# One of four tiles of the second layer normalisation moved to GpSimd, with new instruction orders at both ends

## The chip, the core and the metric

The kernel runs on one core of a Trainium2 chip, as one program with five engines: TensorE (PE, whose weight loads are shown apart as PEld), VectorE (DVE), ScalarE (ACT), GpSimd (POOL) and SyncE (SP, which here only starts DMAs). The metric is the device time of one execution in microseconds; smaller is better. The kernel before took 207.63 us (median of 3 runs, 207.59 to 209.21).

## What is computed

One layer with two halves. Every token (8 batches x 1024 tokens, 128 features, fp32) is normalised over its features, scaled and shifted by columns that depend on the batch, sent through a gated state-space layer and added back. The sum is normalised a second time, scaled and shifted again, and sent through eight experts that are mixed by a router.

```python
h = _layernorm(x) * (1 + ca) + sa
v, gate = split(h @ W_in + b_in);  y = sigmoid(gate) * scan(v) * C     # scan: h = decay * h + v over the tokens
x = x + ga * (y @ W_out + b_out)
h = _layernorm(x) * (1 + cb) + sb
w = softmax(h @ gate_w + gate_b); w = w where w >= 0.1, rescaled to sum 1
x = x + gb * sum_e w[:, e] * (h @ expert_w[e] + expert_b[e])
```

## The kernel before

**Tiling.** The 8192 tokens are cut into 16 groups (g = 0 to 15) of 512 tokens, each of four tiles of 128 tokens (j or t = 0 to 3). A batch is two groups. Groups run as a software pipeline: while the experts of group s are computed, the state-space part of group s + 2 and the second normalisation of group s + 1 are made.

**What each engine does for a group.**
- POOL: `first_norm` (L490, four tiles `xn1` = (x - mean) * rstd), `biased_input` (L454, adds the output bias to `x_in`), `weight_parts` (L501, L504), three `fold`s (L511) and two `add_pairs` (L519), which halve the eight weighed expert outputs `z` to four and then to two.
- ACT: `h1` (L691), `gate` (L699), `exponentials` (L711), `second_norm` (L735, four tiles of `xn2` = `x1` * rstd + shift), `parts_out` (L729), `h2_high` (L707), and `weigh` (L722): seven of the eight half-tiles k of the experts' products, four instructions of 128x128 each, scaled by the router's weight and written from PSUM to `z`.
- DVE: statistics of both normalisations (L961, L968, L984, L986), the inverse root (`root`, L996 to L1026), the router (L1049 to L1075), `scan` (L1101), `gated` (L1110), `first_residual` (L1119, which writes `x1`), `low_part` (L1125), the eighth half-tile (`weigh_onto`, L1087), `sum_pairs` (L1144: adds the last two parts of `z`, both in SBUF, two instructions a group), and `add_bias`, `times_gb`, `result` (L1151, L1158, L1164).
- PE: transposes of `xn1` into `bank_a` and of `xn2` into `bank_g` (both L1789), `gate_input`, `state_input` (L1834, L1828), `output_product` (L1843), `logits` (L1876 to L1880) and eight `half`s of three matmuls of 512 columns (L1903 to L1905) into four PSUM banks, `ring[0]` to `ring[3]`, in turn. `keep_clock` issues n matmuls of the identity that nobody reads, at the start alone.

**What sets the order.** There is no scheduler: each engine's program is a list of calls written out by hand, and every dependence is a semaphore wait in the called function. An engine issues in that order, so that a waiting instruction holds back all behind it on its engine. Groups up to 5 and from 11 on are written out call by call; those between are a loop over s (`for s in range(5, 11)` on POOL, `range(6, 12)` on ACT and PE, `range(6, 11)` on DVE). The order in which the halves use the four ring banks is the list FIRST_HALVES + loop + LAST_HALVES, and `weigh` and `half` follow it.

**The place of the change.** `second_norm(g)` on ACT waits for `shift_ready` of group g, runs its four tiles and raises `xn2_ready`; `turn_xn2(g)` on PE waits for that, and `h2_high(g)` (ACT), `low_part(g)` (DVE), `logits(g)` and the halves of group g (PE) come behind it.

## Times and profile before

| | |
|---|---|
| median of the runs | 207.63 us |
| profiled execution: its own time | 207.48 us |
| its span (first to last instruction) | 205.6 us |
| busy: PE, DVE, ACT, POOL | 93%, 93%, 87%, 81% |
| mean granted TensorE clock | 0.988 of full |

The own time is the span and 1.9 us around it. A row of the timeline gives the start, the length, the engine, the source line, what is written from what, and how many instructions are merged in it; in brackets the engine's idle time ahead of it and what ended it. Instructions of one engine overlap: an instruction's own length is longer than the distance from its start to the next one's, and that distance is what it costs the engine. Distances between starts are therefore used where an engine is full.

### The profile page before, as it was taken

The numbers are of one execution on the slowest core, as the hardware profiler recorded it, in microseconds if no ns is written. First come the engines' busy times: TensorE is split into PE (matmuls) and PEld (weight loads), VectorE is DVE, ScalarE is ACT, GpSimd is POOL, SyncE is SP. The second block draws the span as 40 slices with busy tenths as digits, with TensorE's granted clock in tenths as the row PEclk, the third lists the DMA queues.
The fourth block names the chain that finished last, engine by engine and source line by source line (L and its number), as shares of the span: only waits on it lengthen the run. The fifth ranks groups of instructions, "written<-read, shape, count | busy, mean of one in ns | idle before, by whom it ended". The sixth has DMA issues, their size and how long they took to land.

```text
span 205.6 us, 4254 instructions
## 1 busy us (share of the span) xinstructions
PE 191.5 (93%) x969; PEld 143.3 (70%) x969; DVE 190.3 (93%) x842; ACT 179.1 (87%) x594; POOL 166.3 (81%) x215
## 2 busy tenths in 40 slices
PE   7889999999999999999999999999999999999940
PEld 6643768677777678686868777777868686777720
DVE  3998898999999999999999999999999989898994
ACT  6254449999999999999999999999999999999940
POOL 6169786999879988979898988888997879677950
PEclk9999999999999999999999999999999999999995
DMA  6711111311110111121111201111010101001103
GB/s 196 210 38 51 35 32 49 83 54 51 51 34 19 56 51 51 51 54 53 53 53 45 59 3 50 51 56 51 2 51 3 51 2 53 3 2 51 33 20 102
DMA packets 20114, 10.34 MB, mean 50 GB/s; under 512 B 1369, under 2 KB 19938, under 8 KB 20090
## 3 DMA queue, kind: packets, MB, share of 16 engines
q1 hardware_dynamic: 20072, 10.07, 17.2%
q8 instruction: 8, 0.13, 0.3%
q14 instruction: 16, 0.13, 0.2%
q10 hardware_dynamic: 18, 0.00, 0.0%
HBM read 5.81 MB, written 4.26 MB: 49 GB/s over the span
## 4 chain that ended last, share of the span: by engine, by line
PE 47%; ACT 35%; DVE 10%; issue 5%; DMA 1%; DVEq 0%; ACTq 0%
ACT z L722 23%; PE ring L1903 7%; PE ring L1905 7%; PE ring L1904 7%; ACT xn L735 6%; PE bank_g L1834 4%; PE bank_v L1828 4%; PE bank_a L1843 4%; ACT h_t L691 2%; PE bank_g L1789 2%; PE bank_a L1789 2%; PE bank_g L1880 2%; PE bank_g L1879 2%; ACT bank_g L699 2%; ACT h_hi L707 1%
## 5 line engine op out<-in xcount | busy, mean ns | idle before, releaser
L722 ACT ACTIVATE z<-ring,wts 128x128 f32<-128x128 f32 x436 | 122.1, 423 | 1.3 <-PE ring L1905 0.7
L511 POOL TENSOR_TENSOR z<-z 128x512 f32<-128x512 f32 x45 | 58.5, 1301 | 14.5 <-ACT z L722 14.4
L1903 PE MATMUL ring<-expert_w_hi,h_hi 128*128 128x512 f32 x128 | 60.5, 473 | 0.3 <-ACT z L722 0.3
L1905 PE MATMUL ring<-expert_w_hi,h_lo 128*128 128x512 f32 x128 | 50.5, 395 | 0.0
L1904 PE MATMUL ring<-expert_w_lo,h_hi 128*128 128x512 f32 x128 | 50.4, 394 | 0.0
L519 POOL TENSOR_TENSOR z<-z 128x512 f32<-128x512 f32 x31 | 39.6, 1296 | 7.0 <-DVE z L1087 6.6
L490 POOL TENSOR_SCALAR xn<-x_in,neg_mean,rstd 128x128 f32<-128x128 f32 x60 | 26.3, 452 | 8.6 <-DVE rstd L1026 8.6
L1903 PEld LDWEIGHTS ring<-expert_w_hi,h_hi 128*128 128x128 f32 x128 | 24.2, 189 | 9.2 <-issue 5.6
L1904 PEld LDWEIGHTS ring<-expert_w_lo,h_hi 128*128 128x128 f32 x128 | 24.2, 189 | 7.4 <-issue 4.1
L1905 PEld LDWEIGHTS ring<-expert_w_hi,h_lo 128*128 128x128 f32 x128 | 24.1, 188 | 5.6
L735 ACT ACTIVATE xn<-x,shift,rstd 128x128 f32<-128x128 f32 x60 | 25.6, 554 | 0.0
L1087 DVE SCALAR_TENSOR_TENSOR z<-ring,wts,z 128x128 f32<-128x128 f32 x76 | 23.6, 343 | 0.0
L454 POOL TENSOR_TENSOR x_in<-x_in,gab_all 128x512 f32<-128x512 f32 x16 | 20.6, 1292 | 0.0
L1843 PEld LDWEIGHTS bank_a<-w_outg,y_t 128*128 128x128 f32 x128 | 15.6, 191 | 5.9 <-issue 5.9
L1843 PE MATMUL bank_a<-w_outg,y_t 128*128 128x128 f32 x128 | 17.8, 282 | 0.7 <-DVE y_t L1110 0.4
L1834 PE MATMUL bank_g<-h_t,w_in 128*128 128x512 f32 x32 | 16.6, 599 | 0.6 <-DVE scratch L1037 0.5
L1828 PE MATMUL bank_v<-h_t,w_in 128*128 128x512 f32 x32 | 16.5, 594 | 0.4 <-ACT h_t L691 0.4
L961 DVE BATCH_NORM_STATS2 bn<-x_in 128x6 f32<-128x128 f32 x64 | 16.2, 282 | 0.2 <-DMA x_in<-in_L_attn_x_dram 0.2
L691 ACT ACTIVATE h_t<-bank_a,mod_cols 128x512 f32<-128x512 f32 x16 | 13.4, 838 | 2.1 <-DVE mod_cols L922 1.6
L1880 PE MATMUL bank_g<-gate_w_parts,h_lo 128*128 128x16 f32 x64 | 14.8, 256 | 0.0
L1879 PE MATMUL bank_g<-gate_w_parts,h_hi 128*128 128x16 f32 x64 | 14.8, 256 | 0.0
L699 ACT ACTIVATE bank_g<-bank_g,b_gate_half 128x512 f32<-128x512 f32 x16 | 11.4, 710 | 3.3 <-PE bank_g L1834 3.3
(125 smaller groups left out, 383.6 us busy)
## 6 DMA issues: line engine op xcount, KB each, us to landing
x_in<-in_L_attn_x_dram SPq DMA_DIRECT2D x16, 256.0 KB, 2.9
out_dram<-x SPq DMA_DIRECT2D x15, 256.0 KB, 2.3
expert_w<-in_L_ffn_expert_w_dram SPq DMA_DIRECT2D x2, 256.0 KB, 3.5
wmod<-in_L_wmod_dram SPq DMA_DIRECT2D x1, 384.0 KB, 3.4
expert_b_parts<-b_hi SPq DMA_DIRECT2D x8, 32.0 KB
out_dram<-x SPq DMA_DIRECT2D x2, 128.0 KB, 1.9
w_in<-in_L_attn_W_in_dram SPq DMA_DIRECT2D x1, 128.0 KB, 4.0
expert_b_parts<-b_lo SPq DMA_DIRECT2D x4, 32.0 KB
```

What stands on the lines that cost most here:

```text
L490: last = nc.gpsimd.tensor_scalar(tile(xn1, g % 2, j), tile(x_in, g % SLOTS, j), neg_mean[:, g % 2, col:col + 1], rstd[:, g % 2, col:col + ...
L511: nc.gpsimd.tensor_tensor(z[:, g % 2, t, 0:4, :], z[:, g % 2, t, 0:4, :], z[:, g % 2, t, 4:8, :], ALU.add).then_inc(folded[t], 1)
L519: nc.gpsimd.tensor_tensor(z[:, g % 2, pair, 0:2, :], z[:, g % 2, pair, 0:2, :], z[:, g % 2, pair, 2:4, :], ALU.add).then_inc(pairs_added[i ...
L722: last = nc.scalar.activation(z[:, g % 2, t, e, :], bank_k[:, (e % 4) * P:(e % 4 + 1) * P], ACT.Copy, scale=wts[:, g % 2, t, e:e + 1])
L735: last = nc.scalar.activation(tile(xn2, g % 2, j), tile(x1, g % SLOTS, j), ACT.Identity, bias=shift[:, g % 2, j:j + 1], scale=rstd[:, g % ...
L1087: ins = vec.scalar_tensor_tensor(out=z[:, g % 2, t, n, :], in0=bank_k[:, n * P:(n + 1) * P], scalar=wts[:, g % 2, t, 4 + n:5 + n], in1=z[: ...
L1828: mm(bank_v[:, :], w_in[:, 0:P], h1_t[:, g % 2, :], start=False, stop=True).then_inc(v_ready, 1)
L1834: mm(bank_g[:, :], w_in[:, P:2 * P], h1_t[:, g % 2, :], start=True, stop=True).then_inc(g_ready, 1)
L1843: last = mm(bank_a[:, j * P:(j + 1) * P], tile(y_t, g % 2, j), w_outg[:, b, :], start=True, stop=True)
L1903: mm(bank_k[:, :], hi, expert_w_hi[:, cols], start=True, stop=False)
L1904: mm(bank_k[:, :], hi, expert_w_lo[:, cols], start=False, stop=False)
L1905: mm(bank_k[:, :], lo, expert_w_hi[:, cols], start=False, stop=True).then_inc(e_ready[k], 1)
```

## The change

1. **The split.** For groups 1 to 13 ACT leaves out tile 2 of `second_norm`; POOL computes it by `tensor_scalar`, as (x1 + neg_mean) * rstd, in a new function. PE's `turn_xn2` waits for both engines. Groups 0, 14 and 15 are as before.

```diff
+SPLIT_TILE = 2
+SPLIT_NORMS = range(1, 14)
...
+            def second_norm_tile(g):
+                col = SPLIT_TILE
+                pool.wait_ge(rstd_ready, g + 3)
+                pool.wait_ge(mean_ready, g + 3)
+                nc.gpsimd.tensor_scalar(
+                    tile(xn2, g % 2, col), tile(x1, g % SLOTS, col), neg_mean[:, g % 2, col:col + 1],
+                    rstd[:, g % 2, col:col + 1], ALU.add, ALU.mult).then_inc(xn2_tile_ready, 1)
...
                 for j in range(TILES):
+                    if j == SPLIT_TILE and g in SPLIT_NORMS:
+                        continue
                     last = nc.scalar.activation(
...
             def turn_xn2(g):
                 pe.wait_ge(xn2_ready, g + 1)
+                if g in SPLIT_NORMS:
+                    pe.wait_ge(xn2_tile_ready, g - SPLIT_NORMS[0] + 1)
```

2. **New orders.** The loops on ACT, PE and DVE now run over s = 6 to 9 (`HALF_STEPS = (6, 10)`) and POOL's over 5 to 8, and keep their order inside, but for the new call on POOL. What comes before and behind them is written anew on all four engines: the halves and their weighing, the roots and the router on DVE, the folds on POOL. A line of the table of halves, and the loop of POOL:

```diff
-HALF_STEPS = (6, 12)
+HALF_STEPS = (6, 10)
...
-            for s in range(5, 11):
+            for s in range(5, 9):
                 fold(s, 1)
                 biased_input(s + 3)
                 weight_parts(s)
                 fold(s, 2)
                 first_norm(s + 4)
+                second_norm_tile(s + 2)
                 fold(s, 0)
                 add_pairs(s, 1)
                 add_pairs(s, 0)
```

POOL in the middle of the program, one turn of the loop of before (L511 is `fold`, L490 `first_norm`, L519 `add_pairs`, L454 `biased_input`):

```order
L511 TENSOR_TENSOR z<-z 128x512
L490 TENSOR_SCALAR xn<-x_in,neg_mean,rstd 128x128 x4
L511 TENSOR_TENSOR z<-z 128x512
L519 TENSOR_TENSOR z<-z 128x2x256 x2
L511 TENSOR_TENSOR z<-z 128x512
L454 TENSOR_TENSOR x_in<-x_in,gab_all 128x512
```

The same place in the changed kernel (the functions stand some lines lower in the file; L504 is the new call):

```order
L524 TENSOR_TENSOR z<-z 128x512
L495 TENSOR_SCALAR xn<-x_in,neg_mean,rstd 128x128 x4
L504 TENSOR_SCALAR xn<-x,neg_mean,rstd 128x128
L524 TENSOR_TENSOR z<-z 128x512
L532 TENSOR_TENSOR z<-z 128x2x256 x2
L524 TENSOR_TENSOR z<-z 128x512
L459 TENSOR_TENSOR x_in<-x_in,gab_all 128x512
```

One instruction is added between `first_norm` and the third fold; nothing else in the turn has moved.

3. **The start.** PE's matmuls that nobody reads go to `ring[3]` after a wait for `gb_ready`, and there are eight in place of five ahead of `turn_xn1(2)`. `gates_out(3)` moves on ACT ahead of the bias rows. PE before, around the first second-half transpose (L1776 is `keep_clock`, L1789 a transpose, L1876 the first matmul of `logits(0)`):

```order
L1843 MATMUL bank_a<-w_outg,y_t 128x128 x4
L1776 MATMUL bank_g<-ident 128x128 x4
L1789 MATMUL bank_g<-ident,xn 128x128 x4
L1776 MATMUL bank_a<-ident 128x128 x5
L1789 MATMUL bank_a<-ident,xn 128x128 x4
L1876 MATMUL bank_g<-gate_b_parts,pick 128x64
```

and in the changed kernel:

```order
L1949 MATMUL bank_a<-w_outg,y_t 128x128 x4
L1882 MATMUL ring<-ident 128x128 x4
L1895 MATMUL bank_g<-ident,xn 128x128 x4
L1882 MATMUL ring<-ident 128x128 x8
L1895 MATMUL bank_a<-ident,xn 128x128 x4
L1984 MATMUL bank_g<-gate_b_parts,pick 128x64
```

Three more unread matmuls stand ahead of the transpose of `xn1` of group 2.

4. **The end.** `last_result(1)` on DVE moves from the last place to ahead of `result(14)`, and `times_gb(12)`, `result(12)` move ahead of `low_part(15)`:

```diff
             weigh_onto(15, 3, 3)
-            last_bias(1)
+            last_times_gb(1)
             times_gb(14)
-            last_times_gb(1)
+            last_result(1)
             result(14)
             sum_pairs(15, 0)
             last_bias(0)
             last_times_gb(0)
             last_result(0)
-            last_result(1)
```

## Rows read from the trace of the kernel before

**Rows 1.** The page: busy time with its share, and the chain's shares.

```profile
PE 191.5 (93%) x969; PEld 143.3 (70%) x969; DVE 190.3 (93%) x842; ACT 179.1 (87%) x594; POOL 166.3 (81%) x215
PE 47%; ACT 35%; DVE 10%; issue 5%; DMA 1%; DVEq 0%; ACTq 0%
```

**Rows 2.** Busy time by stretch: us, then busy us and instructions of each engine.

```profile
core 0: us, PE busy (x) PEld busy (x) DVE busy (x) ACT busy (x) POOL busy (x), PEclk, DMA share, GB/s
59.00:72.00 13.00, 12.26 (x60) 8.81 (x59) 12.45 (x50) 12.23 (x43) 11.88 (x14) 1.00 0.15 43
98.00:111.00 13.00, 12.93 (x71) 10.20 (x72) 12.79 (x58) 12.94 (x45) 11.23 (x14) 1.00 0.15 42
163.00:176.00 13.00, 13.00 (x66) 9.67 (x65) 11.71 (x43) 13.00 (x45) 10.91 (x13) 1.00 0.08 21
```

**Rows 3.** Timeline of ACT: the second norms of groups 1, 6, 8, 9, 14.

```profile
29.96 1.64 ACT L735 ACTIVATE xn<-x,shift,rstd 128x128 f32<-128x128 f32 x4
...
85.93 1.72 ACT L735 ACTIVATE xn<-x,shift,rstd 128x128 f32<-128x128 f32 x4
...
107.78 1.72 ACT L735 ACTIVATE xn<-x,shift,rstd 128x128 f32<-128x128 f32 x4
109.32 1.21 ACT L722 ACTIVATE z<-ring,wts 128x128 f32<-128x128 f32 x4
...
118.85 1.73 ACT L735 ACTIVATE xn<-x,shift,rstd 128x128 f32<-128x128 f32 x4
...
173.80 1.79 ACT L735 ACTIVATE xn<-x,shift,rstd 128x128 f32<-128x128 f32 x4
```

**Rows 4.** Timeline of POOL from 102 us: one turn of its loop.

```profile
102.49 1.45 POOL L511 TENSOR_TENSOR z<-z 128x512 f32<-128x512 f32 x1 [0.43 <-ACT z L722]
...
106.90 1.73 POOL L490 TENSOR_SCALAR xn<-x_in,neg_mean,rstd 128x128 f32<-128x128 f32 x4
108.60 1.27 POOL L511 TENSOR_TENSOR z<-z 128x512 f32<-128x512 f32 x1
110.54 2.54 POOL L519 TENSOR_TENSOR z<-z 128x512 f32<-128x512 f32 x2 [0.66 <-DVE z L1087]
113.52 1.43 POOL L511 TENSOR_TENSOR z<-z 128x512 f32<-128x512 f32 x1 [0.44 <-ACT z L722]
```

**Rows 5.** Waits between 98 and 109 us: total us, times, longest.

```profile
PEld bank_v L1824 <- DVE x L1164: 0.7, 1, 0.7
DVE hs L1101 <- PE bank_v L1828: 0.2, 1, 0.2
```

**Rows 6.** Timeline of PE: the transposes of xn2 of group 8.

```profile
109.99 0.60 PE L1789 MATMUL bank_g<-ident,xn 128*128 128x128 f32 x4
```

**Rows 7.** DVE's sum_pairs: durations of all 32; two timeline rows; POOL beside one.

```profile
L1144 DVE TENSOR_TENSOR mix<-z x32: 405/416/1493, 45.1 to 200.9; 128x256 f32<-128x256 f32 x32
...
68.02 1.82 DVE L1144 TENSOR_TENSOR mix<-z 128x256 f32<-128x256 f32 x2
...
113.08 0.74 DVE L1144 TENSOR_TENSOR mix<-z 128x256 f32<-128x256 f32 x2
113.73 0.17 DVE L996 TENSOR_SCALAR scratch<-scratch 128x8 f32<-128x8 f32 x1
...
68.09 1.46 POOL L454 TENSOR_TENSOR x_in<-x_in,gab_all 128x512 f32<-128x512 f32 x1
```

**Rows 8.** Timeline of PE at the start: unread matmuls, transposes, first logits matmul.

```profile
24.26 1.28 PE L1776 MATMUL bank_a<-ident 128*128 128x128 f32 x10
25.38 0.60 PE L1789 MATMUL bank_a<-ident,xn 128*128 128x128 f32 x4
26.14 0.27 PE L1876 MATMUL bank_g<-gate_b_parts,pick 96*128 96x64 f32 x1 [0.16 <-DVE h_lo L1125]
```

**Rows 9.** Timeline of DVE and POOL at the end.

```profile
200.33 0.69 DVE L1164 TENSOR_TENSOR x<-bank_v,x 128x512 f32<-128x512 f32 x1
200.93 0.42 DVE L1144 TENSOR_TENSOR mix<-z 128x256 f32<-128x256 f32 x1
...
202.38 0.76 DVE L1200 TENSOR_TENSOR x<-bank_a,x 128x256 f32<-128x256 f32 x2
...
199.30 1.26 POOL L519 TENSOR_TENSOR z<-z 128x512 f32<-128x512 f32 x1 [0.27 <-DVE z L1087]
```

More of the change, by code:

```diff
@@ L831, in _ @@
             h2_high(6)
-            for s in range(6, 12):
+            for s in range(6, 10):
                 weigh(s - 1, 2)
@@ L845, in _ @@
                 h2_high(s + 1)
+            weigh(9, 2)
+            weigh(9, 3)
+            weigh(9, 5)
+            h1(12)
+            weigh(9, 4)
+            exponentials(10)
+            weigh(9, 0)
+            weigh(9, 1)
+            gate(12)
+            second_norm(11)
+            weigh(10, 6)
+            h2_high(11)
+            parts_out(9)
+            weigh(10, 2)
+            h1(13)
+            weigh(10, 5)
+            weigh(10, 3)
+            weigh(10, 4)
+            exponentials(11)
+            weigh(10, 1)
+            gate(13)
+            weigh(10, 0)
+            second_norm(12)
+            weigh(11, 6)
+            parts_out(10)
+            h2_high(12)
             weigh(11, 2)
             weigh(11, 3)
+            weigh(11, 4)
             weigh(11, 5)
             h1(14)
-            weigh(11, 4)
             exponentials(12)
+            weigh(11, 1)
             weigh(11, 0)
-            weigh(11, 1)
             gate(14)
@@ L1519, in _ @@
             root(7, 0)
-            for s in range(6, 11):
+            for s in range(6, 10):
                 add_bias(s - 2)
@@ L1559, in _ @@
                 root(s + 2, 0)
+            add_bias(8)
+            root(11, 1)
+            logit_sum(10)
+            root(11, 2)
+            router(10, 0)
+            times_gb(8)
+            router(10, 1)
+            result(8)
+            root(11, 3)
+            root(11, 4)
+            x_stats(14, 1)
+            router(10, 2)
+            root(11, 5)
+            root(11, 6)
+            root(11, 7)
+            router(10, 3)
+            negated_mean(11)
+            root(11, 8)
+            router(10, 4)
+            x_stats(15, 0)
+            router(10, 5)
+            scan(12)
+            shifts(11)
+            router(10, 6)
+            gated(12)
+            router(10, 7)
+            weigh_onto(9, 7, 0)
+            x_stats(14, 2)
+            weigh_onto(9, 7, 1)
+            weigh_onto(9, 7, 2)
+            weigh_onto(9, 7, 3)
+            first_residual(12)
+            x_stats(14, 3)
+            x1_stats(12)
+            low_part(11)
+            x_stats(15, 1)
+            moments(12)
+            sum_pairs(9, 0)
+            sum_pairs(9, 1)
+            logit_sum(11)
+            root(12, 0)
             add_bias(9)
             root(12, 1)
-            logit_sum(11)
-            root(12, 2)
             router(11, 0)
@@ L2021, in _ @@
             half(2, 3)
-            half(3, 2)
             half(3, 6)
@@ L2025, in _ @@
             turn_parts(2)
+            half(3, 3)
             after_turn(5)
@@ L2060, in _ @@
             logits(5)
-            half(4, 5)
+            half(4, 0)
             after_logits(5)
@@ L2080, in _ @@
             mixed_bias(4)
-            for s in range(6, 12):
+            for s in range(6, 10):
                 after_product(s + 1)
```

567 lines of the change are left out of this document (321 added, 246 removed), and 14 rows, old and new, of tables (FIRST_HALVES, LAST_HALVES).

## Prediction, written before the changed kernel was run

> **What bounds the kernel now.** I read the busy shares first: PE and DVE 93%, ACT 87%, POOL 81% [rows 1]. Shares over the whole span hide that ACT does little in the first 30 us, so the table by stretch comes next. From 98 to 111 us ACT is busy 12.94 of 13 us, PE 12.93, DVE 12.79, POOL 11.23; from 163 to 176 us ACT is busy all 13.00 us while DVE has dropped to 11.71 [rows 2]. Three engines are full at once in the middle, and ACT alone bounds the last groups. The chain gives PE 47% and ACT 35% [rows 1]: it hops between engines that are both full, so a cut on one of them is worth no more than the distance to the next.
>
> The clean measure is the period, from one second normalisation on ACT to the next: 118.85 - 107.78 = 11.07 us [rows 3]. In that time ACT has no idle time that a row names. From group 1 (29.96) to group 14 (173.80) there are 13 periods in 143.84 us, 11.06 us each: five early ones up to 85.93 with 11.19 us each, and eight later ones with 10.98 us [rows 3]. The early groups are not as tight: from 59 to 72 us ACT is busy 12.23 of 13 us only [rows 2].
>
> **The change part by part.**
>
> *ACT.* Four tiles hold ACT from 107.78 to 109.32 [rows 3], 1.54 us, so one tile is 0.385 us. Thirteen tiles go: 5.0 us of ACT's work. ACT's own limit on the period falls from 11.07 to 10.69 us.
>
> *POOL.* Its four tiles of the same kind (`tensor_scalar`, 128x128) hold it from 106.90 to 108.60 [rows 4], 0.43 us each. The new instruction reads `x1` in place of `x_in`, both in SBUF, so I take 0.43 us. A turn of POOL's loop is 113.52 - 102.49 = 11.03 us, and 0.66 + 0.44 = 1.10 us of it is idle [rows 4]: 9.93 us of work, 10.36 us with the tile. That fits under 10.69, but with 0.3 us of room where there was 1.1.
>
> *The added wait on PE.* Behind `turn_xn2` stand the group's logits and halves, so a late tile would hold everything. It would start at about 108.6 and end at about 109.1 in the time of before, in the place of the fold at 108.60 [rows 4]; ACT's last tile ended near 109.5; PE turns them at 109.99 [rows 6]. The tile has 0.9 us of room; I cost the wait at nothing. If POOL is held up by more than that, each us costs a us. The fold and `add_pairs` behind the tile move back by 0.43 us, inside the 0.66 us that POOL waited for DVE ahead of `add_pairs` [rows 4].
>
> *DVE and PE as next bounds.* Nothing is taken from either. DVE is busy 12.79 of 13 us [rows 2]; scaled to the period that is 10.9 us of 11.07, and part of it is short waits of one small instruction for the one before it, which other orders can fill. PE waits 0.7 us for DVE's `result`, and DVE then 0.2 us for PE's state product [rows 5], so PE has some 0.7 us of room: 10.4. The new period thus lies between 10.69 (ACT still bounds) and 11.07 (DVE or POOL leave it where it is). DVE's figure argues for 10.9, ACT's for 10.7; I take 10.80, nearer to ACT's, since the early groups, now at 11.19, have idle time on ACT that DVE's and PE's new orders address. Thirteen periods: 13 x 10.80 = 140.4, against 143.84: **-3.4 us**. Some 1.9 us of it falls to the five early groups, 1.5 us to the eight later ones.
>
> *A rule against the change.* DVE's `sum_pairs` reads two operands from SBUF. Its 32 instructions have a median of 0.416 us and a longest of 1.493 us [rows 7]. The long one is in the pair at 68.02, which took 1.82 us in place of the 0.74 at 113.08; POOL's `biased_input` ran from 68.09 to 69.55 beside it [rows 7]. The extra is 1.08 us of DVE, once in the kernel. In the steady part the pair of 113.08 to 113.73 falls between the end of POOL's `add_pairs` (113.08) and its next fold (113.52) [rows 4, 7], that is, into POOL's idle time, which the new tile eats into. The Trainium skill ("SBUF — State Buffer", section "Who interferes with whom") says that a DVE instruction with two SBUF inputs and a GpSimd instruction that reads SBUF exclude each other, and that the later one waits until the earlier one is through. By that rule the trace agrees for the pair at 68.02, and POOL's own limit would be 10.36 plus the pair's 0.65, about 11.0 us, so that the steady part would gain next to nothing.
>
> *The start.* Five unread matmuls (ten records) take 25.38 - 24.26 = 1.12 us [rows 8]; eight take 1.79, so the transpose moves 0.67 us later, from 25.38 to 26.05. It takes 0.45 us, so `logits(0)` starts at 26.5 in place of 26.14 [rows 8], which waited for `h_lo` before: **+0.35 us** if nothing later absorbs it. The other moves of the start (`gates_out(3)`, the POOL order) are costed at nothing: before, `gates_out(3)` ran in ACT's waits for PE; if it were late, PE's unread matmuls would wait for it. Bounds 0 and +0.7.
>
> *The end.* DVE's last two results take 0.76 us merged, about 0.34 each by distance, from 202.38 [rows 9]. One of them now stands ahead of `result(14)` and the last `sum_pairs`. That one started at 200.93 right after `result(14)` (200.33), with POOL's `add_pairs` done at 200.56 [rows 9]: DVE is the later, so the last chain starts up to 0.34 us later. The two last stores leave SP one after the other anyway, so little comes back at the far end. I take **+0.3 us**, bounds 0 and 0.4. Moving `times_gb(12)` and `result(12)` ahead of `low_part(15)` fills DVE's wait for ACT; costed at nothing.
>
> *Sum.* Against the profiled execution's own 207.48 us: 207.48 - 3.4 + 0.35 + 0.3 = 204.7. The median of the runs is 0.15 above it, so **204.9 us**, 1.3% less.
>
> **The rivals.**
>
> *ACT's cut comes through in full.* The period falls to 10.69 in all groups: 13 x 10.69 = 139.0, -4.9 us; with the start and end at +0.3 together, 207.63 - 4.9 + 0.3 = 203.0; if the early groups also lose their idle time beyond that, 202.5. For it: ACT at 13.00 of 13 us near the end, with DVE at 11.71 [rows 2], where the other engines have room. Against: DVE at 12.79 in the middle.
>
> *The next engine gives it back.* The steady period stays at 11.0, by DVE's load or by POOL that has no room. Only the early groups gain, 0.2 us each, 1.0 us together, and start and end cost 0.6: 207.63 - 1.0 + 0.6 = 207.2. For it: three engines full at once, and POOL's room of 1.1 us shared by the tile (0.43) and the pair (0.65), which makes 1.08.
>
> *POOL and DVE collide (slower).* The place is `sum_pairs` on DVE against the fold or `biased_input` behind `add_pairs` on POOL. With POOL back to back, the pair of each group meets a running POOL instruction. Each collision costs DVE up to 1.08 us, as at 68.02 [rows 7]; DVE has 0.2 us a group to spare. The gain of 3.4 us is used up by three new collisions, and the time passes 209.7 (slower by over 1%) with four to five. With five: 204.9 + 5.4 = 210.3. Against: both engines take their places from the same earlier event. `add_pairs` waits for DVE's `weigh_onto`, and `sum_pairs` comes behind the same instruction on DVE, so the pair's gap follows POOL when DVE is late; the fold behind it waits for ACT's `weigh` (0.44 us) [rows 4], and ACT, though lighter, must still wait for PE's transposes.
>
> **How the numbers follow.** A measurement of this kernel tells about 1% from no change. Forecast (203.6 to 206): 0.42. Full gain (under 203.6): 0.20. Given back (206 to 209.7): 0.27. Collisions (over 209.7): 0.11. The limit for faster by over 1% is 205.6: all of the full gain and 0.37 of the forecast's 0.42, 0.57; the limit for slower is 209.7: 0.11; between them 0.32. The range runs from 202.6 (full gain, with bounds 0 for start and end) to 208.2 (given back, with one collision), and leaves out about 0.04 below and 0.15 above. The forecast's own range is 203.6 to 206.
>
> **What would show each step.** In the profile after: distances between second norms on ACT of 10.7 to 10.9 us, and three tiles in 1.15 us; POOL's new instruction near 0.43 us and ended before PE's transposes of `xn2`, with no wait of those for POOL; POOL's idle time per turn down to 0.3 to 0.7 us; the median of `sum_pairs` still near 0.416 us, with at most one or two long ones; the first half-product some 0.35 us later than before. The prediction is wrong if DVE rather than ACT has no gap left at 11.0 us, if more than three `sum_pairs` pass 1 us, or if the last groups, where ACT alone was full, do not get shorter.

## The result, with the profile after

The changed kernel took 210.38 us (median of 20 executions, 209.03 to 212.39) against 207.68 us for the kernel before beside it (20 executions, 207.51 to 209.34). The ratio is 1.0098 with a 95% interval of [1.0074, 1.0123]: about 1% slower, where 1.3% faster was predicted, and outside the range of 202.6 to 208.2.

The executions of one kernel fall into groups, the lowest of which holds 15 of 20 for the kernel before and 7 of 20 for the changed one, so beside the median I give each kernel's **base**, the median of its executions within 0.5 us of its fastest. The base is 207.63 us before and 209.17 us after: 1.54 us more.

The profiled execution took 212.28 us, 3.1 us above the base, with a span of 210.5 us. Some of what it shows is therefore no part of the base; the profile of the kernel with five unread matmuls in place of eight (below), which was taken at 208.86 us, tells the two apart. Busy time and shares, the granted clock by 40 slices of the span, and the chain by engine, to be read against [rows 1]:

```profile
PE 196.6 (93%) x975; PEld 146.4 (70%) x975; DVE 192.0 (91%) x842; ACT 176.1 (84%) x581; POOL 172.1 (82%) x228
PEclk9999999999987999999999999999999999999995
PE 72%; DVE 23%; issue 2%; ACT 1%; POOL 0%; DVEq 0%; POOLq 0%
```

ACT lost 3.0 us of busy time and nearly vanished from the chain, from 35% to 1%. The time did not follow it: PE took its share. The table by stretch, with the columns of [rows 2] (the third from the end is the mean granted clock):

```profile
59.00:72.00 13.00, 11.94 (x51) 7.90 (x50) 11.02 (x47) 9.85 (x34) 9.83 (x14) 0.87 0.13 36
98.00:111.00 13.00, 13.00 (x63) 9.24 (x62) 12.79 (x64) 12.58 (x45) 12.29 (x17) 1.00 0.17 50
163.00:176.00 13.00, 13.00 (x67) 9.93 (x66) 11.99 (x47) 12.86 (x46) 11.70 (x15) 1.00 0.07 21
```

In the middle PE is at 13.00 of 13 and ACT has come down to 12.58. From 59 to 72 us no engine is full, and the granted clock is below 1. ACT's timeline, the second norms of groups 1 to 7, 9 and 14, against [rows 3]:

```profile
31.99 1.26 ACT L776 ACTIVATE xn<-x,shift,rstd 128x128 f32<-128x128 f32 x3
42.78 1.32 ACT L776 ACTIVATE xn<-x,shift,rstd 128x128 f32<-128x128 f32 x3
53.61 1.26 ACT L776 ACTIVATE xn<-x,shift,rstd 128x128 f32<-128x128 f32 x3
67.57 1.27 ACT L776 ACTIVATE xn<-x,shift,rstd 128x128 f32<-128x128 f32 x3
79.69 1.27 ACT L776 ACTIVATE xn<-x,shift,rstd 128x128 f32<-128x128 f32 x3
90.31 1.31 ACT L776 ACTIVATE xn<-x,shift,rstd 128x128 f32<-128x128 f32 x3
101.19 1.35 ACT L776 ACTIVATE xn<-x,shift,rstd 128x128 f32<-128x128 f32 x3
...
123.17 1.34 ACT L776 ACTIVATE xn<-x,shift,rstd 128x128 f32<-128x128 f32 x3
...
177.85 1.81 ACT L776 ACTIVATE xn<-x,shift,rstd 128x128 f32<-128x128 f32 x4
```

Group 1 comes 2.0 us later than before (29.96). Groups 6 to 14 take 177.85 - 90.31 = 87.54 us, against 87.87 before [rows 3]: the eight later periods gained 0.33 us together, where 1.5 had been predicted. The loss lies between groups 3 and 5: two steps of 13.96 and 12.12 us, against 11.34 and 11.65 before. In the profile with five unread matmuls they are 12.28 and 12.36 us, so some 1.4 us of the two belong to this one execution.

What happens there is in DVE's and POOL's timelines:

```profile
58.23 1.27 POOL L459 TENSOR_TENSOR x_in<-x_in,gab_all 128x512 f32<-128x512 f32 x1
...
58.33 1.83 DVE L1211 TENSOR_TENSOR mix<-z 128x256 f32<-128x256 f32 x2
...
61.59 0.22 DVE L1104 TENSOR_REDUCE scratch<-bank_g 128x32 f32<-128x64 f32 x1
...
72.27 1.27 POOL L459 TENSOR_TENSOR x_in<-x_in,gab_all 128x512 f32<-128x512 f32 x1
...
72.47 1.68 DVE L1211 TENSOR_TENSOR mix<-z 128x256 f32<-128x256 f32 x2
```

L459 is `biased_input`, L1211 `sum_pairs`. A pair of `sum_pairs` that runs alone takes 0.74 us [rows 7]; these two took 1.83 and 1.68 us. In both, POOL's instruction had started 0.1 to 0.2 us earlier, and the pair ended 0.6 to 0.7 us after POOL's end (58.23 + 1.27 = 59.50 and 58.33 + 1.83 = 60.16; 72.27 + 1.27 = 73.54 and 72.47 + 1.68 = 74.15), about the time of a pair that runs alone. I call this a meeting. Of all 32 `sum_pairs` of the changed kernel, two are over 1 us; the kernel before had one [rows 7]. The first meeting is new: the change puts `biased_input(5)` right behind `add_pairs`. The second is the one that the kernel before had at 68 us: `biased_input(6)` stands behind `weight_parts(3)` in both kernels. The durations over the span:

```profile
L1211 DVE TENSOR_TENSOR mix<-z x32: 400/415/1457, 47.1 to 205.8; 128x256 f32<-128x256 f32 x32
```

The Trainium skill ("SBUF — State Buffer", section "Who interferes with whom") says that these two kinds of instruction exclude each other and that the later waits for the earlier. By that rule the trace agrees, in each of the meetings shown here.

Behind the first meeting DVE's `logit_sum` (L1104, 61.59) is late, and PE waits for it. PE's timeline; L1940 is `gate_input`:

```profile
61.87 1.93 PE L1940 MATMUL bank_g<-h_t,w_in 128*128 128x512 f32 x2 [1.06 <-DVE scratch L1104]
...
75.18 1.13 PE L1940 MATMUL bank_g<-h_t,w_in 128*128 128x512 f32 x2 [0.29 <-DVE scratch L1104]
```

PE stood still for 1.06 us, and in this execution its next matmuls took 1.93 us a pair in place of 1.13: the granted clock was at the lower level, 1.2 GHz, from about 62 to 65.5 us. The two stretches of 4 us there:

```profile
59.00:63.00 4.00, 2.94 (x16) 1.95 (x14) 3.98 (x16) 2.82 (x11) 2.43 (x4) 0.88 0.00 0
63.00:67.00 4.00, 4.00 (x10) 2.03 (x9) 2.33 (x10) 2.03 (x8) 3.40 (x6) 0.69 0.23 66
```

POOL's tile and loop are as the prediction had them. All 13 new instructions by duration, and from a loop turn of POOL, against [rows 4]:

```profile
L504 POOL TENSOR_SCALAR xn<-x,neg_mean,rstd x13: 438/447/450, 31.6 to 168.3; 128x128 f32<-128x128 f32 x13
```

```profile
111.21 1.74 POOL L495 TENSOR_SCALAR xn<-x_in,neg_mean,rstd 128x128 f32<-128x128 f32 x4
112.93 0.45 POOL L504 TENSOR_SCALAR xn<-x,neg_mean,rstd 128x128 f32<-128x128 f32 x1
113.34 1.27 POOL L524 TENSOR_TENSOR z<-z 128x512 f32<-128x512 f32 x1
114.85 2.54 POOL L532 TENSOR_TENSOR z<-z 128x512 f32<-128x512 f32 x2 [0.23 <-DVE z L1154]
117.83 1.44 POOL L524 TENSOR_TENSOR z<-z 128x512 f32<-128x512 f32 x1 [0.44 <-ACT z L761]
```

The tile takes 0.45 us, POOL's waits of 0.66 and 0.44 us have become 0.23 and 0.44, and nothing in the loop collides.

PE's start, against [rows 8]:

```profile
26.03 1.95 PE L1882 MATMUL ring<-ident 128*128 128x128 f32 x16
27.82 0.60 PE L1895 MATMUL bank_a<-ident,xn 128*128 128x128 f32 x4
```

Eight unread matmuls cost 27.82 - 26.03 = 1.79 us, as worked out. That is 0.67 us more than the five of before. Group 1 is 2.03 us late in this one execution, though, and most of it was lost earlier, where both kernels run the same work. The first transposes of `xn1` on PE in the changed kernel, and in the kernel before:

```profile
8.20 1.12 PE L1895 MATMUL bank_a<-ident,xn 128*128 128x128 f32 x4
```

```profile
7.59 0.66 PE L1789 MATMUL bank_a<-ident,xn 128*128 128x128 f32 x4 [0.22 <-DVE xn L1209]
```

The same four transposes took 1.12 us in place of 0.66. The granted clock reads 1.00 in this stretch in both, so it does not tell the two apart; other kernels with the old start show the long form too (1.12 us with the split in the early groups alone, 0.66 us with the split in all). The five other profiled executions with the long form took 1.4 to 1.7 us more than the base of their kernel. It comes and goes between executions and is no part of the change.

### The profile page after: what moved, and what is told of

Same layout as the page of the kernel before. It is cut to its first block, busy times and chain, and to the rows that moved or that the text cites. A ratio compares the mean times of both kernels' runs of the same rounds, so it can differ in the third digit from the quotient of the medians.

```text
span 210.5 us, 4281 instructions
## 1 busy us (share of the span) xinstructions
PE 196.6 (93%) x975; PEld 146.4 (70%) x975; DVE 192.0 (91%) x842; ACT 176.1 (84%) x581; POOL 172.1 (82%) x228
## 4 chain that ended last, share of the span: by engine, by line
PE 72%; DVE 23%; issue 2%; ACT 1%; POOL 0%; DVEq 0%; POOLq 0%
PE ring L2011 10%; PE ring L2012 10%; PE ring L2013 10%; PE bank_a L1949 7%; PE bank_v L1934 7%; PE bank_g L1940 6%; PE ring L1882 4%; PE bank_a L1895 3%; PE bank_g L1988 3%; PE bank_g L1987 2%; DVE mix L1211 2%; DVE hs L1168 2%; PE bank_g L1895 2%; PE bank_v L1930 2%; DVE bn L1035 2%
## 5 line engine op out<-in xcount | busy, mean ns | idle before, releaser
L532 POOL TENSOR_TENSOR z<-z 128x512 f32<-128x512 f32 x31 | 39.4, 1288 | 3.7 <-DVE z L1154 3.3
L776 ACT ACTIVATE xn<-x,shift,rstd 128x128 f32<-128x128 f32 x47 | 20.6, 553 | 0.1
L459 POOL TENSOR_TENSOR x_in<-x_in,gab_all 128x512 f32<-128x512 f32 x16 | 20.6, 1289 | 0.0
L1940 PE MATMUL bank_g<-h_t,w_in 128*128 128x512 f32 x32 | 18.7, 668 | 1.3 <-DVE scratch L1104 1.3
L1934 PE MATMUL bank_v<-h_t,w_in 128*128 128x512 f32 x32 | 18.0, 647 | 0.5 <-ACT h_t L730 0.5
```

The lines of the kernel that those rows point to most:

```text
L532: nc.gpsimd.tensor_tensor(z[:, g % 2, pair, 0:2, :], z[:, g % 2, pair, 0:2, :], z[:, g % 2, pair, 2:4, :], ALU.add).then_inc(pairs_added[i ...
L1934: mm(bank_v[:, :], w_in[:, 0:P], h1_t[:, g % 2, :], start=False, stop=True).then_inc(v_ready, 1)
L1940: mm(bank_g[:, :], w_in[:, P:2 * P], h1_t[:, g % 2, :], start=True, stop=True).then_inc(g_ready, 1)
```

## The experiments

**One part of the change alone.** The first two kernels take the change apart: the new orders with `second_norm` whole on ACT, and the old orders with the split. In the second, the new call stands behind `first_norm` in each of POOL's groups:

```diff
             first_norm(6)
+            second_norm_tile(4)
             fold(2, 1)
```

> The changed kernel with its new orders, but all four tiles of every second normalisation on ACT, none on POOL. Theory A (the orders lose the time: POOL's biased_input now stands right behind add_pairs in groups 1 and 2, and meets DVE's sum_pairs): still slower than the kernel before, 209 us or more, and sum_pairs still has two or three instructions over 1 us. Theory B (the split loses it, through POOL's extra instruction or PE's extra wait): back at 207 to 208 us. Theory C (the orders were made for the split and both are needed): slower than the changed kernel, 211 to 213.

Measured: 209.94 us (four executions, all within 0.2 us), ratio 1.0101 [1.0062, 1.0140].

> The kernel before, its orders untouched, with the split alone: POOL computes tile 2 of groups 1 to 13 right behind first_norm. Theory A (orders lose): at or a little under the kernel before, 206.5 to 207.6. Theory B (split loses): slower, 208.5 to 210. The forecast's rival of a full gain for ACT: 203. If DVE and not ACT sets the period of 11.0 us in the middle, the gain is under 1 us, since nothing of DVE's work went away; ACT then shows idle time of some 0.3 us a group where it had none.

Measured: 206.05 us, base 205.96, ratio 0.9921 [0.9891, 0.9950]. The split alone gains 1.65 us of base; the orders alone lose 2.3 us. The durations of `sum_pairs` in the two kernels, orders alone first:

```profile
L1201 DVE TENSOR_TENSOR mix<-z x32: 413/420/1491, 45.4 to 203.3; 128x256 f32<-128x256 f32 x32
```

```profile
L1165 DVE TENSOR_TENSOR mix<-z x32: 406/418/500, 45.0 to 199.4; 128x256 f32<-128x256 f32 x32
```

The orders alone have three long pairs (1.88, 1.57 and 1.52 us at 45, 58 and 70 us), the split alone has none. The long pairs at 58 and 70 us are the two meetings of the changed kernel; the one at 45 us runs beside `biased_input(4)`. The new orders are the loss, and with the old orders the split is a gain, though half of the predicted 3.4 us and more than the expectation's "under 1 us". With the new orders it is worth less, 209.94 - 209.17 = 0.8 us of base, on four executions of the one, and by the medians (209.94 and 210.38 us) nothing.

**The meetings of the changed kernel.** POOL's `biased_input` of groups 5 and 6 is moved behind the next fold, away from DVE's pairs at 58 and 72 us:

```diff
-            biased_input(5)
             weight_parts(2)
             fold(2, 0)
+            biased_input(5)
...
             weight_parts(3)
-            biased_input(6)
             fold(3, 1)
+            biased_input(6)
```

> The changed kernel, POOL's order in groups 2 and 3 alone altered: biased_input(5) and biased_input(6) stand behind the next fold, not between add_pairs and it. Theory A: both long sum_pairs (1.46 us at 58 us and 1.35 us at 72 us of the changed kernel's profile) are at 0.42 us; PE's wait of 1.06 us for the logit sum goes, and with it the stretch of 3.4 us at half clock behind it: 1.5 to 2.5 us less than the changed kernel's median, 208 to 209, and TensorE's mean clock at 0.986 or more in every run. Theory B (the half-clock stretch has another cause): the long ones go, the clock stays at 0.98 in most runs, under 1 us gained.

Measured: 208.38 us, base 207.38, ratio 1.0001 [0.9968, 1.0034]. The base falls by 1.8 us, PE does not wait at 61 us, and the steps of groups 3 to 5 are 11.26 us each, where the kernel with five unread matmuls has 12.28 and 12.36: 2.1 us for the two meetings. The mean clock was 0.986 or more in six of ten executions, not in all as theory A had it. And a smaller meeting came up, of the next pair with POOL's second `add_pairs` (L532):

```profile
78.18 2.53 POOL L532 TENSOR_TENSOR z<-z 128x512 f32<-128x512 f32 x2
...
80.12 1.28 DVE L1211 TENSOR_TENSOR mix<-z 128x256 f32<-128x256 f32 x2
```

The step from group 5 to 6 is 11.14 us there, against 10.61 in the kernel with five unread matmuls, so this meeting hides 0.5 us of what the edit gained. The meetings were the largest part of the loss; 1.4 us against the split alone stayed, with that 0.5 us in it.

**The unread matmuls.** `keep_clock(ring[3], 8)` becomes `keep_clock(ring[3], 5)` in the changed kernel.

> The changed kernel with five in place of eight unread matmuls ahead of the transpose of group 2. If the three more cost what they take (0.67 us, of which 0.35 us reach the logits): 0.3 to 0.7 us less than the changed kernel. If they are hidden by the wait for h_lo: no change. If they keep the clock up at the start: a later start of the full clock in more runs, and more time than the changed kernel.

Measured: 210.63 us (four executions), ratio 1.0127 [1.0062, 1.0191]. Its four executions lie in four different groups, at clocks of 0.989, 0.980, 0.972 and 0.981; against the changed kernel's groups with the same clocks they are 0.3, 0.1, 0.45 and 0.3 us lower. So the three matmuls cost about 0.3 us, as predicted (+0.35), on four executions only. Its profile was taken at its fastest execution and has both meetings (pairs of 1.84 us at 56.39 and 1.92 us at 68.86) and the same wait of PE, with a granted clock of 1.00 from 59 to 67 us:

```profile
59.94 1.12 PE L1940 MATMUL bank_g<-h_t,w_in 128*128 128x512 f32 x2 [1.06 <-DVE scratch L1104]
```

From the second norm of group 1 to that of group 7 it takes 67.73 us, the split alone 64.87. The two steps with the meetings are 24.64 against 21.39 us, 3.25 more; the other four are 0.39 us less. So the loss of the early orders stands in these two steps, and 1.1 us of it stays there when the meetings are gone (11.26 + 11.26 = 22.52 us).

**Old early orders, new late ones.** With the split: orders of before up to the loop, of the change behind it.

> The split, with the orders of before up to the middle loops and those of the changed kernel from the loops on. Tells what the new late orders are worth with the split. If they are as good as the old ones: equal to the split alone (206.0). In the changed kernel's profile, the periods of groups 11 to 14 are 0.9 us shorter in sum than with the split alone, and the one from 14 to 15 and the tail 0.9 us longer: so 205.7 to 206.5 is expected, and the whole loss of the changed kernel lies in its early orders.

Measured: 206.23 us, base 206.02, ratio 0.9926 [0.9889, 0.9963], the same as the split alone. All of the loss is in the orders of the early groups, the start included.

**The tail.** The same kernel with DVE's last calls in the old order, `last_result(1)` behind `last_result(0)`:

```diff
-            last_result(1)
             result(14)
             sum_pairs(15, 0)
             last_bias(0)
             last_times_gb(0)
             last_result(0)
+            last_result(1)
```

> The split, the early orders of before and the new late orders (which took 206.0), with DVE's last twelve calls in the order of before: last_result(1) behind last_result(0) again. Prediction's step: the new tail costs 0.3 us, so 205.7. Rival: what DVE gains behind the last sum_pairs pays for it, 206.0 +- 0.1; the last store leaves 2.9 us before the end with the new tail and 2.5 with the old.

Measured: 206.13 us (four executions), ratio 0.9899 [0.9850, 0.9948], base 205.68 from two executions against 206.02: 0.3 us, on few executions. The step "+0.3 us for the end" is not contradicted, nor is it sharp.

**A meeting added to, and one taken from, the kernel before.** First `biased_input(5)` is put ahead of `weight_parts(2)`, as in the changed kernel:

```diff
+            biased_input(5)
             weight_parts(2)
             fold(2, 0)
-            biased_input(5)
```

> The kernel before with one POOL instruction moved: biased_input(5) ahead of weight_parts(2), as in the changed kernel. It then runs from 56.2 to 57.5 us, across the place of DVE's sum_pairs of group 1 (56.81). If a meeting costs what the long ones took: sum_pairs waits for the rest of it, 0.6 us, and the kernel is 0.4 to 1.1 us slower, with one more long sum_pairs in its profile. If sum_pairs is only slow there by chance, nothing changes.

Measured: 208.97 us, base 207.91, ratio 1.0031 [0.9994, 1.0067], so 0.35 us more of base, just under the expected 0.4; the interval of the ratio still holds 1. The step from group 3 to 4 is 11.72 us, 0.38 more than before. POOL's and DVE's timelines (L454 is `biased_input`, L1144 `sum_pairs`):

```profile
57.84 1.27 POOL L454 TENSOR_TENSOR x_in<-x_in,gab_all 128x512 f32<-128x512 f32 x1
...
58.47 1.30 DVE L1144 TENSOR_TENSOR mix<-z 128x256 f32<-128x256 f32 x2
```

The pair came in the middle of POOL's instruction, was 0.56 us too long, and ended again 0.66 us after POOL's end (59.11 to 59.77). A meeting costs DVE what is left of POOL's instruction, not a fixed 1.08 us. In the meeting at 68.02 us [rows 7] the pair started ahead of POOL, so that only its second instruction (1.493 us) stood: it ended at 69.84 us, 0.29 us after POOL's end at 69.55.

Then DVE's pair of group 2 is put ahead of the aggregates, so that it is through before POOL's `biased_input` at 68.1 us:

```diff
-            moments(5)
             sum_pairs(2, 1)
             sum_pairs(2, 0)
+            moments(5)
```

> The kernel before, without the split, with DVE's two sum_pairs of group 2 ahead of the aggregates (moments) of group 5, so that the pair runs at 67.4 to 68.2 us, before POOL's biased_input starts at 68.1. Theory A (each meeting costs its full 1.08 us of path, and most of the split's 1.65 us is that it moved this one away): the step from group 4 to 5 falls from 11.65 to 10.6 us, time 206.6 against 207.6. Theory B (ACT's work in the early groups is what the split saved): at most 0.3 us, 207.3 to 207.7. In between: both carry part.

Measured: 206.83 us, base 206.82, ratio 0.9947 [0.9919, 0.9974]: 0.85 us less than the kernel before, without any split. The durations, and the second norms of groups 4 and 5 on ACT (10.74 us apart, 11.65 before):

```profile
L1144 DVE TENSOR_TENSOR mix<-z x32: 405/415/452, 45.2 to 200.3; 128x256 f32<-128x256 f32 x32
```

```profile
63.62 1.65 ACT L735 ACTIVATE xn<-x,shift,rstd 128x128 f32<-128x128 f32 x4
74.36 1.79 ACT L735 ACTIVATE xn<-x,shift,rstd 128x128 f32<-128x128 f32 x4
```

So the meeting that [rows 7] showed was a cost of 0.85 us in the kernel before, and the split alone had removed it by accident, by bringing DVE's pair to 67.0 us. That is half of the split's gain. It also falls between the two theories: one meeting carries half.

**Where the split gains.** The old orders with the split in groups 1 to 6 alone, and in groups 7 to 13 alone (`SPLIT_NORMS = range(1, 7)` and `range(7, 14)`):

> The orders of before, the split in groups 1 to 6 alone. Theory A (the gain of the split is made in the early groups, by waits and one meeting, and none in the later ones): 205.5 to 206.1, as with the split in 13 groups (205.95) or lower, since the step into group 14 stays 10.63 in place of 11.13. Theory B (each group carries its share of ACT's time, 0.385 us): half the gain, 206.8.

Measured: 205.65 us, base 205.65, ratio 0.9882 [0.9835, 0.9930].

> The orders of before, the split in groups 7 to 13 alone. Theory A: 207.4 to 208.0, no gain at all or a loss of up to 0.5 us by the step into group 14. Theory B (a share for each group): 206.7. The prediction had put 1.5 us of gain in the eight later groups.

Measured: 208.58 us, base 208.12, ratio 1.0024 [0.9992, 1.0057].

The early groups gain 2.0 us, the late ones lose 0.45 us. Both rows that explain it can be read. In the kernel before, PE waits for ACT's second norm in groups 2, 3 and 4 and nowhere else; its timeline:

```profile
42.60 0.63 PE L1789 MATMUL bank_g<-ident,xn 128*128 128x128 f32 x4 [0.49 <-ACT xn L735]
53.96 0.63 PE L1789 MATMUL bank_g<-ident,xn 128*128 128x128 f32 x4 [0.31 <-ACT xn L735]
65.30 0.63 PE L1789 MATMUL bank_g<-ident,xn 128*128 128x128 f32 x4 [0.21 <-ACT xn L735]
```

These are 1.01 us together. With the 0.85 us of the meeting that makes 1.86 of the 2.0 us. Two runs bear this out: the kernel before without its meeting still has the three waits, the one with the early split has none of them, and their bases differ by 206.82 - 205.65 = 1.17 us, of which the steps between groups 2 and 5 make 1.13 (33.48 and 32.35 us). In the kernel with the late split PE has one new wait, for POOL's tile of group 13; PE's timeline and POOL's:

```profile
166.56 0.63 PE L1804 MATMUL bank_g<-ident,xn 128*128 128x128 f32 x4 [0.49 <-POOL xn L502]
...
165.95 0.46 POOL L502 TENSOR_SCALAR xn<-x,neg_mean,rstd 128x128 f32<-128x128 f32 x1
```

The step from group 13 to 14 grew from 10.63 to 11.16 us, about the 0.45 us of the base. The tile stands there behind `first_norm(15)`; in the changed kernel it stands ahead of it, and PE does not wait. The six steps before it, from group 7 to 13, take 66.28 us with three tiles on ACT and took 66.30 with four: the split gained nothing there. The kernel with the early split beats both kernels: 205.65 us against 207.72 us beside it.

**What bounds the middle.** These runs leave out part of the computation in five middle groups, from DVE, from PE or from both, with the split and without it. From DVE the statistics of two of four tiles go:

```diff
-                x_stats(s + 4, 1)
...
-                x_stats(s + 4, 2)
```

> The kernel before with the split alone, and two of the four x_stats of a group left out in the five turns of DVE's middle loop (groups 10 to 14 are then normalised with a part of an older group's statistics). That takes 0.39 us of DVE's work from each of five periods and nothing from ACT, PE or POOL. If DVE sets the middle period once ACT is relieved: those five periods shrink from 11.0 to 10.6 or 10.7, 1.5 to 1.9 us less than the split alone. If PE's own work, or ACT's new limit of 10.7, sets it: less than 0.7 us gained.

Measured: 205.22 us, base 205.21, ratio 0.9871 [0.9809, 0.9932]: 0.75 us of the 1.95 us that the cut takes from DVE by distance (five times 0.39), so DVE was not the only bound either.

> The kernel before with the same two x_stats of a group left out in the same five turns. If ACT bounds the kernel before, as the prediction has it (no idle time in a period of 11.07 us): no change, at most 0.3 us. If DVE alone bounds it: 1.5 to 1.9 us less. If both are full at the same 11.0 us: no gain here, but a gain in the kernel with the split.

Measured: 206.85 us, base 206.71, ratio 0.9971 [0.9932, 1.0009]. With all four tiles on ACT the cut on DVE still gave 0.9 us: ACT alone did not bound these groups.

From PE the second of three matmuls of two halves goes:

```diff
+                if not (6 <= g <= 10 and k in (3, 5)):
-                mm(bank_k[:, :], hi, expert_w_lo[:, cols], start=False, stop=False)
+                    mm(bank_k[:, :], hi, expert_w_lo[:, cols], start=False, stop=False)
```

> The orders of before with the split tile, and PE's two matmuls of halves 3 and 5 left out in groups 6 to 10 (part of the computation; 0.46 us of PE a group), DVE whole. Theory A (DVE, about 11.0 us of work a period, is the first of two full engines, PE at 10.87 the second): relieving PE alone gives at most 0.3 us over the kernel, 205.7 to 206.1 against 206.0 of the split alone. Theory B (PE is the first bound): periods of those groups at 10.7, time 205.0.

Measured: 205.91 us, base 205.86, ratio 0.9922 [0.9896, 0.9949]: 0.1 us.

> The orders of before with the split tile, two x_stats of DVE left out in each of five middle turns (0.55 us of DVE a group) and two matmuls of 512 columns of PE left out for halves 3 and 5 of groups 6 to 10 (0.46 us of PE a group); both leave out part of the computation. With the cut on DVE alone the five periods were 10.67 to 10.95, mean 10.86, and the time 205.2. Theory A (PE, busy 10.94 to 11.00 of 11 us there, is the floor once DVE is relieved, and ACT's own limit with the split is 10.69): periods 10.5 to 10.7 us in those groups, time 204.4 +- 0.3. Theory B (ACT or POOL is the floor at 10.87 already): periods stay at 10.85, time 205.2.

Measured: 205.76 us, base 205.00 from two executions, ratio 0.9897 [0.9853, 0.9942]. The periods of groups 8 to 12 are 10.78 to 10.91 us, nearer to theory B.

> The kernel before (no split), with both cuts of e10: two x_stats of DVE a group and two matmuls of PE a group in five middle groups (part of the computation). Here ACT has all four tiles. Theory A (ACT's own limit lies at 11.07 us a period, as the prediction took it): periods stay at 11.0, time 207.5. Theory B (ACT's limit is 10.69 + 0.385 at most, but its busy time holds slack, since the cut on DVE alone brought the periods to 10.93): periods 10.8 to 10.9 and time 206.5 +- 0.3; the split would then be worth 0.15 to 0.3 us a group with the other two engines out of the way, which e10 against this run gives.

Measured: 206.48 us, base 206.46, ratio 0.9940 [0.9914, 0.9966], as theory B had it.

At last both cuts about twice as large, four statistics (two of them those of the second normalisation) and four matmuls a group:

> The orders of before with the split; in five middle groups four statistics instructions of DVE (1.1 us a group) and four matmuls of 512 columns of PE (0.92 us a group) are left out, which is part of the computation. Theory A (PE and DVE were still the floor after the smaller cut): periods of these groups at 10.5 to 10.65 us, ACT's own limit with three tiles. Theory B (the floor of 10.81 is ACT or POOL or the chain between them): periods stay at 10.75 to 10.85.

Measured: 204.85 us, base 204.42 from two executions, ratio 0.9843 [0.9792, 0.9894].

> The same cuts without the split. Theory A: periods at 10.8 to 10.9 us, ACT full at its own limit with four tiles, so that the split would be worth 0.2 to 0.35 us a group there. Theory B (the same floor for both): the same periods as with the split.

Measured: 206.01 us, base 205.97, ratio 0.9932 [0.9899, 0.9965].

| left out in five groups (busy time) | base with split | base without | difference |
|---|---|---|---|
| nothing | 205.96 | 207.6 | 1.65 |
| DVE 0.55 us a group (0.39 by distance) | 205.21 | 206.71 | 1.5 |
| DVE 0.55, PE 0.46 | 205.00 | 206.46 | 1.45 |
| DVE 1.1, PE 0.92 | 204.42 | 205.97 | 1.55 |

The split is worth nearly the same whatever is taken from the other engines, so its worth does not lie in the groups that were relieved. The periods themselves say it; second norms of groups 8 and 12 and the stretch from 105 to 148 us (columns of [rows 2]), twice the cut with the split:

```profile
107.15 1.46 ACT L756 ACTIVATE xn<-x,shift,rstd 128x128 f32<-128x128 f32 x3
...
150.02 1.46 ACT L756 ACTIVATE xn<-x,shift,rstd 128x128 f32<-128x128 f32 x3
```

```profile
105.00:148.00 43.00, 41.33 (x209) 30.05 (x209) 41.78 (x182) 42.67 (x147) 40.50 (x53) 1.00 0.16 44
```

and without it:

```profile
107.55 1.83 ACT L735 ACTIVATE xn<-x,shift,rstd 128x128 f32<-128x128 f32 x4
...
150.43 2.01 ACT L735 ACTIVATE xn<-x,shift,rstd 128x128 f32<-128x128 f32 x4
```

```profile
105.00:148.00 43.00, 40.77 (x209) 30.18 (x208) 41.49 (x183) 43.00 (x151) 38.76 (x49) 1.00 0.16 44
```

Four periods take 42.87 us with three tiles and 42.88 us with four, 10.72 each. Without the split ACT is busy 43.00 of 43 us and yet turns in 10.72 us, where the kernel before needed 11.07 with ACT at 12.94 of 13 [rows 2, 3]. A busy share of 99% was therefore no proof that ACT was full: at least 0.35 us of its 11.07 us was slack that stood inside the lengths of its instructions. What holds both versions at 10.72 us after the double cut is not settled. One difference shows: with the split, DVE's pairs in these five turns take 0.92 to 1.13 us in place of 0.74, which would fit short meetings with a POOL that is busy 40.50 of 43 us.

**Filling PE's wait.** In the changed kernel, PE's `half(2, 3)` is moved ahead of the logits that wait for `logit_sum`:

```diff
             logits(3)
             half(2, 7)
+            half(2, 3)
             after_logits(3)
...
             state_input(5)
-            half(2, 3)
```

> The changed kernel, with PE's half(2, 3) moved from behind to ahead of the logits that wait for DVE's late logit_sum, so that about 0.6 us of PE's 1.06 us of waiting at 61 us is filled; the late sum_pairs stays (one L1211 near 58 us at about 1.45 us). Theory A (the wait of PE at 61 us is what the half-clock stretch of 3.4 us behind it needs): no stretch of granted clock at half near 62 us, most executions with a mean clock of .985 or more, median 209.1 +- 0.3 against 210.4 of the changed kernel. Theory B (the lower clock in many executions comes by chance and has nothing to do with the wait): the median stays at 210 to 210.8 and mean clocks of .98 are as frequent as before. In both the fastest executions stay near 209.0, since the meeting of sum_pairs and biased_input is still there.

Measured: 209.84 us (seven executions), base 209.15, ratio 1.0080 [1.0044, 1.0116]. PE's timeline, and the stretch of 4 us that had a clock of 0.69:

```profile
61.81 1.12 PE L1940 MATMUL bank_g<-h_t,w_in 128*128 128x512 f32 x2 [0.21 <-DVE scratch L1104]
...
65.39 0.31 PE L2017 MATMUL bank_v<-ident,w_parts 128*96 128x128 f32 x1 [0.68 <-DVE hs L1168]
```

```profile
63.00:67.00 4.00, 3.32 (x15) 1.92 (x14) 3.97 (x17) 3.90 (x14) 3.73 (x7) 1.00 0.23 66
```

The wait shrank to 0.21 us, but the later `state_input` made PE wait 0.68 us for `scan` instead, and the base did not move. A filled wait on PE gave nothing while DVE stayed late.

**The clock.** The lower clock behind the wait shows in the changed kernel's profile, and not in that of the kernel with five unread matmuls, which had the same wait of 1.06 us. So a wait of this length can be followed by the lower level, but need not be. In the executions, 7 of 20 of the changed kernel lie 2 us or more above its base, and none of the seven with the filled wait (its highest is 1.55 us above); three of those seven still lie 0.7 us above at a mean clock of 0.983. The median of 209.84 us lies between what the two theories expected, 209.1 and 210 to 210.8. I take it as pointing to the wait as the cause of the highest groups, on seven executions; it is not shown. A lower clock also comes without that wait: in the profiles of the kernel without the two meetings and of the one with the old tail it is 0.50 in each us from 10 to 13, and these executions took 1.1 and 0.9 us more than their base. In the us from 8 to 9 PE was busy 0.71 and 0.48 us there, but also 0.48 in the kernel before, whose clock stayed at 1.00; what lets it fall is open.

## Why the prediction was wrong

**The meetings.** The prediction named the mechanism of the loss as a rival, "POOL and DVE collide", with a chance of 0.11, and looked for it in the loop. There it did not happen: POOL's turns show no long `sum_pairs`. It happened in the written-out groups. One meeting is new, where the diff puts `biased_input(5)` right behind `add_pairs`; the other is the old one of [rows 7], which the split alone had removed and the new orders kept. In neither did DVE wait ahead of the pair (its instruction before ran to 58.41 and 72.56 us), so no common event started the two engines: their lists only brought both instructions to the same time. That the rival's figure of 210.3 us is near the measured 210.38 is luck, since it was made of five collisions on top of a gain of 3.4 us. The step that failed is the costing of the new orders: the sum had +0.35 and +0.3 us for start and end, and nothing for groups 2 to 7. Measured at the base, the orders cost 3.2 us on top of the split: 1.8 for the meetings (2.1 by the two steps), about 0.3 for the unread matmuls, about nothing for the late orders, tail included, and the rest, 0.8 to 1.1 us, in the other new orders of the early groups, which no run took apart.

**The gain of the split.** It was sized at 3.4 us, 1.5 of them in the later groups. It measured 1.65 us: +2.0 early, -0.45 late. The step that failed is "ACT's own limit on the period falls from 11.07 to 10.69". 11.07 was not ACT's limit. The run with the double cut had ACT at four tiles in 10.72 us. Two periods of the middle take 123.17 - 101.19 = 21.98 us in the changed kernel, and the same two took 118.85 - 96.87 = 21.98 us before:

```profile
96.87 1.72 ACT L735 ACTIVATE xn<-x,shift,rstd 128x128 f32<-128x128 f32 x4
```

ACT's relief turned into idle time on ACT (busy 12.58 of 13 us, 12.94 before). The busy share of the last groups, 13.00 of 13 us, was read in the same wrong way: the step from group 13 to 14 took 10.62 us with three tiles and 10.63 with four. That is the third of the prediction's own signs of being wrong. The first came in part: at periods of 10.99 us ACT had gaps, while DVE was busy 12.79 and PE 13.00 of 13 us.

**The early groups.** They do gain, 2.0 us with the old orders, where 1.9 was predicted with the new ones, but by another mechanism: three waits of PE that name ACT's `xn` (1.01 us) and one meeting (0.85 us). Both stood in the trace of before. The wait of PE for `xn` was the row to look for, since it is the only one that the split can shorten.

**DVE's and PE's room.** DVE's 10.9 us argued for a period of 10.9, and this was the better argument: the cut on DVE alone took the time down by 0.75 to 0.9 us with and without the split, though that is less than half of the 1.95 us cut. PE alone relieved gave 0.1 us, which agrees with the prediction that PE was not the bound; how much room it had, that run does not measure. With DVE relieved as well, the cut on PE gave 0.2 us more.

**The added wait on PE.** Costed at nothing, and right in the changed kernel, where no transpose waits for POOL. In the old orders it cost 0.49 us at group 13. The tile's own duration (0.43 predicted, 0.45 measured), the unread matmuls (1.79 us) and POOL's waits (0.66 to 0.23) were right.

**The price of a meeting.** "Up to 1.08 us each" was about right as a bound: the steps that held the meetings of the changed kernel were 1.0 and 1.1 us longer (0.9 each by the base, with the smaller meeting that came in their place), the one before cost 0.85, and two partial ones 0.35 and 0.5. "Three new ones use up the gain" was wrong, since it counted against a gain of 3.4 us. Against 1.65 us, one new meeting, one kept, and the other early orders were enough. The prediction also read the steady pair of 113.08 to 113.73 us as lying in POOL's idle time. POOL's next fold started at 113.52, 0.2 us before the pair was through, and took 1.43 us in place of the 1.27 at 108.60 [rows 4, 7].

**The range.** Its lower and upper ends both rested on the size of ACT's cut; the upper one, 207.2 us with one collision of 1.08, comes to 208.3, still below the result. A case in which the new orders cost by themselves, without POOL being full, was not in it.

## What to carry to other kernels

Before work is taken from a busy engine, look for the wait, on the engine that is paced by it, which names the tile that would come earlier. Between groups 7 and 13, where no such wait stood, taking work off ACT alone gained nothing (66.28 against 66.30 us), whatever its busy share. And when an order is written anew, lay the two timelines side by side: where an instruction of DVE with two operands in SBUF and one of POOL come to the same time, as behind `add_pairs` here, look for a DVE duration far above its median, and move one of the two.

## What the runs showed of the hardware

- Where POOL's `tensor_tensor` had started first, the DVE pair ended 0.61 to 0.66 us after POOL's end, in each of three cases read closely (at 60.16, 74.15 and 59.77 us); where the pair had started first, only its second instruction stood, and the pair ended 0.29 us after (at 69.84 us). The loss is the rest of POOL's instruction, and most of it reached the kernel's time: 0.85 us of 1.08 in the kernel before.
- An instruction's length on ACT can hold slack that no row calls idle: busy 43.00 of 43 us at periods of 10.72 us, and 12.94 of 13 us at periods of 11.07 us, with all four tiles on ACT in both.
- PE's granted clock went to the lower level for about 3.4 us behind a wait of 1.06 us in one profiled execution, and stayed at the upper level behind the same wait in another.
- The same four transposes at 8 us took 0.66 us in some profiled executions and 1.12 in others, with a granted clock of 1.00 in both; executions with the long form took 1.4 to 1.7 us more than the base of their kernel.
